# The step size's two halves: one read of PSUM each, and the absolute value made from the copy ahead of the exponent

## The chip, the core and the metric

The kernel runs on one core of one Trainium2 chip. The metric is the device time of one execution, in microseconds (us). Five engines work side by side, each through its own list of instructions in order: TensorE (PE in the profile; its weight loads are PEld), VectorE (DVE), ScalarE (ACT), GpSimd (POOL) and SyncE (SP), which issues most of the transfers. They wait for each other through semaphores.

## The reference

Input `x` is 32 sequences of 256 tokens with 128 channels. Each token goes through a mixture-of-experts layer, a selective-scan layer and the same mixture-of-experts layer again:

```
x = x + 0.5 * ffn(layernorm(x))
x = x + mamba(layernorm(x))
x = x + 0.5 * ffn(layernorm(x))

# in mamba
delta = softplus(x_conv @ W_dt + b_dt)            # 256 inner channels: the step size
dA    = exp(delta * A)                            # 16 states
h     = dA * h + (delta * x_conv) * B             # over the 256 tokens, one after the other
y     = sum over states of h * C, + D_skip * x_conv
```

`ffn` has 8 experts with hidden width 176, of which each token uses the best two, and a shared expert of width 352. The 256 inner channels of mamba lie on 128 partitions in two halves. softplus is computed as max(v, 0) + ln(1 + exp(-|v|)).

## The kernel before, in words

Two sequences (512 tokens) make a group, and there are 16 groups. The function `body(k, odd)` of every engine is one step of a software pipeline; k runs from -2 to 17. In step k group k is scanned; group k+1 goes through normalisation, projections, convolution and step size (the steps that `lead` lets in); group k+2 enters with its first ffn; and group k-1 leaves the scan and starts on its second. A step has 32 slots. The table `PLAN` says which named step stands in which slot, and every engine walks through the same table and takes its own part of each named step, so the table and the order of the `if`s within `body` are the order of each engine's list. In slot 2s VectorE scans state s of the 16 (L924, `hist`), from the decays that ScalarE made (L686, four instructions for two states) and from an input term that VectorE multiplied in PSUM (L876, `ps_db`) out of a row that TensorE spread there (L1058). GpSimd multiplies each `hist` by the row C (L623, `prod`), and one transfer per two states adds `prod` to `yacc` (L640). Between these stand 28 units of the two ffn passes: TensorE L1076 (`ps_h1a`, `ps_h1b` in turn), ScalarE's Silu L706, TensorE L1098 (`ps_h2`), VectorE's product L904 with a row of expert weights (`wrow`) that SyncE loads (L418), GpSimd's product L555, TensorE's down projection L1090. TensorE's matmul L1076 of a unit waits until the Silu two units earlier is done, since it writes the same bank. The second pass's last unit ends in VectorE's L911 (named step `addy1`, slot 21), which adds `ps_y` to `xres`; SyncE then stores the finished group (L384), waits until the store has landed, loads a new group (L376), and goes on with the expert rows.

A group's small products share one PSUM bank, `ps_m`. TensorE may write it only after the engine that last took it has counted up `misc_taken` (`claim`). Among these are `dt0` (slot 17) and `dt1` (slot 18), the two halves of the step size (L1141). ScalarE takes each half from the bank twice, and the second read gives the bank free:

```
774  nc.scalar.activation(dtmp[:, half, :], ps_m[:], ACT.Abs,
775                       bias=b_dt_c[:, half:half + 1]).then_inc(softplus_chain, 1)
776  nc.scalar.activation(dpre[:, half, :], ps_m[:], ACT.Identity,
777                       bias=b_dt_c[:, half:half + 1]).then_inc(misc_taken, 1)
```

In slot 20, behind the decays of states 12 and 13, comes `sp_exp`, which needs the same table of functions as the decays:

```
794  act.wait_ge(softplus_chain, (HALVES + 1) * (k + 2) - 1)
795  nc.scalar.activation(dtmp[:], dtmp[:], ACT.Exp, scale=-1.0).then_inc(softplus_chain, 1)
```

`sp_ln` (slot 22, L780) takes the logarithm, and VectorE joins `dpre` and `dtmp` to `delta` in slot 26 (L965). The units of the first ffn pass stand in slots 18 to 31, one in each, from position 0; position 3 is in slot 21 (`ps_h1b`), position 5 in slot 23 (`ps_h1b`). Slot 23 also holds the transposition of the normalised tokens for the second pass (`xT1`: TensorE L1037, ScalarE's copy L711), and slot 24 the routing product (`logits1`, TensorE L1110), which VectorE copies in slot 25 (L944) before it ranks the experts. In the first steps (k below 2) another table, `START_PLAN`, is used.

Of the kernel before, what the change touches and what calls it, by code (L numbers as in the profile page):

```python
# [17 lines left out]
def macaron_kernel(nc, x, W_in, b_in, conv_w, conv_b, W_xp, b_xp, W_dt, b_dt, A_log, D_skip, W_out, b_out,  # L18
# [6 lines left out]
    E, _, H = W1.shape  # L25
# [19 lines left out]
    NW = 4  # L45
# [31 lines left out]
    MISC_ENTRY = ["xT0", "logits0", "wT0"]  # L77
    MISC_LEAD = ["xT2", "in0", "in1", "in2", "in3", "dt0", "dt1", "xproj", "cT", "bT"]
    MISC_TAIL = ["outproj", "xT1", "logits1", "wT1"]
# [13 lines left out]
    def start(k):  # L93
        return isinstance(k, int) and k < FULL

    def plan(k):
        return START_PLAN if start(k) else PLAN

    def sp_plan(k):
        return START_SP if start(k) else SP_PLAN  # L100

    SETUP_MADE, SETUP_TAPS, SETUP_EDGE = 16, 24, 28

    def first(k):
        return isinstance(k, int) and k == -2

    def enters(k):
        return not isinstance(k, int) or 0 <= k + 2 < G

    def lead(k):  # L110
        return not isinstance(k, int) or 0 <= k + 1 < G

    def scans(k):
        return not isinstance(k, int) or 0 <= k < G

    def tail(k):
        return not isinstance(k, int) or 0 <= k - 1 < G

    def last(k):
        return not isinstance(k, int) or 0 <= k - 2 < G  # L120

    def misc_list(k):
        names = (enters(k) * MISC_ENTRY) + (lead(k) * MISC_LEAD) + (tail(k) * MISC_TAIL)
        return [n for s in range(SLOTS) for n in plan(k).get(s, []) if n in names]

    def before(k, names_of):

        if isinstance(k, int):
            return sum(len(names_of(i)) for i in range(-2, k))
        return sum(len(names_of(i)) for i in range(-2, FULL)) + (k - FULL) * len(names_of(FULL))  # L130

    def turn(k, name):

        return before(k, misc_list) + misc_list(k).index(name) + 1

    def turn_last(k, name):

        after = misc_list(k - 1 if isinstance(k, int) else FULL - 1)
        return before(k, misc_list) - (len(after) - 1 - after.index(name))

    def ffn_no(k, f):

        if isinstance(k, int) and k < FULL:
            return k + 2
        if isinstance(k, int) and k >= G - 2:
            return k + G - 2
        return 2 * k + 1 - f

    def route_no(k, step):

        if isinstance(k, int) and k < 1:
            return k + 2
        if isinstance(k, int) and k >= G - 2:
            return k + G - 1
        return 2 * k + (2 if step.endswith("1") else 1)

    def fcount(k, f, per, n):

        return ffn_no(k, f) * per + n

    def f_parity(k, f):
        return ffn_no(k, f) % 2 if isinstance(k, int) else 1 - f

    def w_turn(k, odd, f, e):

        if isinstance(k, int):
            n = ECHUNK * ffn_no(k, f) + e
            return n % NW, 2 * 16 * (n // NW + 1)
        n = ECHUNK * (2 * odd + 1 - f) + e
        return n % NW, 2 * 16 * (2 * ECHUNK // NW) * (k - odd) + 2 * 16 * (n // NW + 1) + (  # L170
            2 * 16 * (2 * ECHUNK % NW) // NW) * (k - odd)

    def unit(k, odd, slot, lag):

        back = slot < lag
        of, parity = (k - 1, 1 - odd) if back else (k, odd)
        units = START_UNIT if start(of) else UNIT
        if slot - lag + back * SLOTS not in units:
            return None
        f, pos = units[slot - lag + back * SLOTS]  # L180
        return (of, parity, f, pos) if (last(of) if f else enters(of)) else None

    def home(engine, group):

        return group % XS if isinstance(group, int) else engine.snap(group % XS)

    def iterations(engine, body):

        for k in range(-2, G + 2):
            body(k, k % 2)  # L190

    ctx = ExitStack()
    with ctx:
# [176 lines left out]
        def _(sp):  # L370
            def row_of(g):

                return g * NSEQ if isinstance(g, int) else sp.snap(g * NSEQ)
# [5 lines left out]
            def store(g, slot, first, k):  # L379

                sp.wait_ge(y_taken, ffn_no(k, 1) + 1)

                sp.wait_ge(x_loaded, 16 * min(g + XS, G) if isinstance(k, int) else 16 * (g + XS))
                sp.dma_start(out[bass.ds(first, NSEQ)].rearrange("b (t p) c -> p (b t) c", p=P),  # L384
                             xres[:, slot, :, :]).then_inc(x_stored, 16)
                sp.wait_ge(x_stored, 16 * (g + 1))

            def rows_c(g, par, p):
# [4 lines left out]
                if p > 1 or not isinstance(g, int) or g > 0:  # L393
                    sp.wait_ge(prod_done, NS * g + 2 * p - 2)
# [10 lines left out]
            def rows_w(k, odd, f, e, route=None):  # L405

                place, value = w_turn(k, odd, f, e)
                n = fcount(k, f, NCHUNK, e if e >= NW else e - (NCHUNK - ECHUNK))
                if not isinstance(n, int) or n > 0:
                    sp.wait_ge(h2_taken, n)  # L410
# [10 lines left out]
            def body(k, odd):  # L421
                for slot in range(SLOTS):
                    for step in sp_plan(k).get(slot, []):
                        if step[0] == "c" and scans(k):
                            rows_c(k, odd, int(step[1:]))
                        elif step == "next_c0" and lead(k):
                            rows_c(k + 1, 1 - odd, 0)
                        elif step == "store_w0" and enters(k) or step == "store_w1" and tail(k):
                            store_w(k, int(step[7]))
                        elif step[:3] == "w0:" and enters(k):  # L430
                            rows_w(k, odd, 0, int(step[3:]), route_no(k, "wT0"))
                        elif step[:3] == "w1:" and int(step[3:]) < NW and tail(k):
                            rows_w(k + 1, 1 - odd, 1, int(step[3:]), route_no(k, "wT1"))
                        elif step[:3] == "w1:" and int(step[3:]) >= NW and last(k):
                            rows_w(k, odd, 1, int(step[3:]))
                        elif step == "keep_x1n" and scans(k):
                            sp.wait_ge(norm_ready[2], k + 1)
                            if tail(k):
                                sp.wait_ge(mamba_added, k)
                            sp.dma_start(rtok[:], x1n[odd][:]).then_inc(x1n_ready, 16)  # L440
                        elif step == "store_x" and last(k):
                            at, stored, loaded = home(sp, k - 2), row_of(k - 2), row_of(k - 2 + XS)
                            store(k - 2, at, stored, k)
                            if not isinstance(k, int) or k - 2 + XS < G:
                                load(k - 2 + XS, at, loaded)
# [25 lines left out]
            iterations(sp, body)  # L471
# [3 lines left out]
        def _(pool):  # L475
# [39 lines left out]
            def norms_list(k):  # L515
# [681 lines left out]
```

## Time and profile before

| | us |
|---|---|
| median of 3 runs | 1838.47 |
| lowest, highest | 1837.09, 1841.13 |
| the profiled execution's own time | 1839.04 |
| its span in the trace | 1837.3 |
| TensorE busy | 1658.7 |
| VectorE busy | 1478.3 |
| GpSimd busy | 1445.7 |
| ScalarE busy | 1266.2 |

The granted clock of TensorE was 0.959 of full speed on average over the span. A timeline row has the start in us from the beginning of the span, the duration, the engine, the line of the kernel, what is written and read (partitions x elements), how many instructions were merged into the row, and in brackets the idle time of that engine before it and who ended it. A releaser is inferred from semaphore events.

### The profile page before, as it was taken

To read this page: it belongs to the slowest core of one execution; us is meant where nothing else is said; L and a number is where in the kernel's file an instruction comes from. 1 tells how busy PE (TensorE), PEld (TensorE's weight loads), DVE (VectorE), ACT (ScalarE), POOL (GpSimd) and SP (SyncE) were. 2 spreads that over 40 slices of the span, in tenths; PEclk is the share of its full clock that TensorE was granted. 3 is DMA by queue.
4 is the path that set the end of the run, shared out by engine and by line. 5 is a ranking of instruction groups with operands and counts; after the bars stand their busy time and mean duration, and the time that the engine had idled before them with its cause. 6 is when DMAs were issued, how large, how long until landed. Compare 5 with 4: busy or idle time off the path is not lost.

```text
span 1837.3 us, 24041 instructions
## 1 busy us (share of the span) xinstructions
PE 1658.7 (90%) x7378; PEld 1001.5 (55%) x7378; DVE 1478.3 (80%) x2241; ACT 1266.2 (69%) x2030; POOL 1445.7 (79%) x1366
## 2 busy tenths in 40 slices
PE   5898788999999999999999999999999999958488
PEld 3454445556555555656555555656555555534255
DVE  1438889989798988989798988989898998989732
ACT  2367678787877778776867777786877777665422
POOL 3336869888898988888888888888898888887753
PEclk9998889999999999999999999999999999969599
DMA  6026768687776868686777867777677868767642
GB/s 158 24 87 141 180 150 193 160 205 173 185 184 162 207 156 201 158 194 170 178 184 170 201 158 189 181 187 184 168 190 172 196 156 192 184 152 186 143 104 69
DMA packets 121287, 304.54 MB, mean 166 GB/s; under 512 B 19299, under 2 KB 40518, under 8 KB 106822
## 3 DMA queue, kind: packets, MB, share of 16 engines
q0 software_dynamic: 18432, 125.84, 34.4%
q1 hardware_dynamic: 98406, 174.46, 33.3%
q10 hardware_dynamic: 4320, 2.71, 0.5%
q8 instruction: 58, 0.95, 0.2%
q14 instruction: 71, 0.58, 0.1%
HBM read 167.67 MB, written 5.24 MB: 94 GB/s over the span
## 4 chain that ended last, share of the span: by engine, by line
POOL 43%; DMA 23%; issue 14%; PE 9%; DVE 7%; ACT 1%; SPq 1%; POOLq 0%; ACTq 0%; DVEq 0%
DMA yacc<-prod 19%; POOL prod L623 18%; POOL gated L555 14%; DVE hist L924 4%; DMA crow<-c_rows 3%; POOL yacc L619 2%; PE ps_y L1090 2%; DVE ps_db L876 2%; POOL yacc L640 1%; PE ps_h1a L1076 1%; SPq L418 1%; PE ps_h2a L1098 1%; PE ps_h1b L1076 1%; PE ps_h2b L1098 1%; POOL xres L610 1%
## 5 line engine op out<-in xcount | busy, mean ns | idle before, releaser
L623 POOL TENSOR_TENSOR prod<-hist,crow 128x1024 f32<-128x1024 f32 x224 | 556.5, 2484 | 204.7 <-DVE hist L924 171.0
L1090 PEld LDWEIGHTS ps_y<-down_w,gated 128*128 128x128 f32 (+1 forms) x3584 | 474.0, 196 | 276.4 <-issue 160.1
L924 DVE TENSOR_TENSOR_SCAN hist<-decay,ps_db 128x1024 f32<-128x1024 f32 x256 | 583.3, 2278 | 2.8
L555 POOL TENSOR_TENSOR gated<-gated,silu 128x512 f32<-128x512 f32 x352 | 493.3, 1450 | 74.4 <-DVE gated L904 71.4
L1090 PE MATMUL ps_y<-down_w,gated 128*128 128x128 f32 (+1 forms) x3584 | 491.8, 282 | 58.0 <-POOL gated L555 56.3
L876 DVE TENSOR_TENSOR ps_db<-du,ps_db 128x1024 f32<-128x1024 f32 x256 | 313.2, 1224 | 114.2 <-PE ps_db L1058 112.1
L686 ACT ACTIVATE decay<-delta,a_neg 128x510 f32<-128x510 f32 x512 | 326.8, 709 | 3.7 <-DVE delta L965 2.2
L706 ACT ACTIVATE silu<-ps_h1a 128x512 f32<-128x512 f32 (+1 forms) x224 | 132.9, 593 | 194.8 <-PE ps_h1a L1076 194.6
L1076 PE MATMUL ps_h1b<-xnT,up_w 128*128 128x512 f32 x448 | 236.7, 610 | 3.6 <-ACT silu L706 3.1
L1098 PE MATMUL ps_h2a<-xnT,up_w 128*128 128x512 f32 (+1 forms) x448 | 236.1, 609 | 1.9 <-DVE gated L904 1.9
L1076 PE MATMUL ps_h1a<-xnT,up_w 128*128 128x512 f32 (+1 forms) x448 | 236.4, 609 | 0.0
L1098 PE MATMUL ps_h2b<-xnT,up_w 128*128 128x512 f32 x448 | 232.0, 600 | 1.4 <-DVE gated L904 1.4
L904 DVE TENSOR_TENSOR gated<-ps_h2b,wrow 128x512 f32<-128x512 f32 x192 | 130.7, 681 | 60.3 <-PE ps_h2b L1098 40.2
L706 ACT ACTIVATE silu<-ps_h1b 128x512 f32<-128x512 f32 x224 | 133.0, 594 | 63.6 <-PE ps_h1b L1076 52.1
L686 ACT ACT_TABLE_LOAD x124 | 159.1, 1283 | 2.2
L904 DVE TENSOR_TENSOR gated<-ps_h2a,wrow 128x512 f32<-128x512 f32 x160 | 107.9, 674 | 46.3 <-PE ps_h2a L1098 36.2
L706 ACT ACT_TABLE_LOAD x111 | 142.4, 1283 | 2.0
L1058 PE MATMUL ps_db<-bT,sel_b 96*128 96x512 bf16 x256 | 102.2, 399 | 41.5 <-DVE hist L924 41.4
L1047 PE MATMUL ps_m<-xnT,w_conv 128*128 128x512 f32 (+3 forms) x256 | 118.2, 596 | 0.0
L1076 PEld LDWEIGHTS ps_h1a<-xnT,up_w 128*128 128x128 f32 (+1 forms) x448 | 85.0, 192 | 56.6 <-issue 47.0
L1076 PEld LDWEIGHTS ps_h1b<-xnT,up_w 128*128 128x128 f32 x448 | 79.1, 194 | 64.0 <-issue 37.5
L640 POOL DMA_DIRECT2D yacc<-prod x112 | 101.6, 908 | 1.6 <-issue 1.3
(136 smaller groups left out, 1937.5 us busy)
## 6 DMA issues: line engine op xcount, KB each, us to landing
yacc<-prod POOLq DMA_DIRECT2D x112, 1024.0 KB, 10.0
crow<-c_rows SPq DMA_DIRECT2D x128, 512.0 KB, 5.0
wrow<-w_rows SPq DMA_DIRECT2D x320, 128.0 KB, 6.3
wrow<-w_rows SPq DMA_DIRECT2D x64, 224.0 KB, 7.0
wrow<-w_rows SPq DMA_DIRECT2D x64, 192.0 KB, 6.4
wrow<-w_rows SPq DMA_DIRECT2D x64, 160.0 KB, 2.9
yacc<-yacc POOLq DMA_DIRECT2D x16, 512.0 KB, 7.8
wrow<-w_rows SPq DMA_DIRECT2D x64, 96.0 KB, 2.9
```

The costliest lines, as they stand in the source:

```text
L555: nc.gpsimd.tensor_tensor(gated[:, pos % NGATE, :], gated[:, pos % NGATE, :], silu[:, (pos + NCHUNK * f_parity(of, f)) % NSILU, :], ALU.mu ...
L623: nc.gpsimd.tensor_tensor(prod[:, (pair - 1 + odd) % 2, s % 2, :, :], hist[:, s % 2, :, :], c_all, ALU.mult).then_inc(prod_done, 1)
L640: pool.dma_start(yacc[odd][:], prod[:, (pair - 1 + odd) % 2, :, :, :], accum_op=ALU.add).then_inc(acc_done, 16)
L686: ins = nc.scalar.activation(decay[:, s % NA, half, :, 1:LEN], d[:, :, 1:LEN], ACT.Exp, scale=a_neg[:, half, s:s + 1])
L706: nc.scalar.activation(silu[0:r, (pos + NCHUNK * f_parity(k, f)) % NSILU, :], ps_h1[pos % 2][0:r, :], ACT.Silu).then_inc(silu_done, 1)
L876: nc.vector.tensor_tensor(ps_db[:].rearrange("p (h t) -> p h t", h=HALVES), du[par][:], ps_db[:, TG:2 * TG].unsqueeze(1).to_broadcast([P, ...
L904: nc.vector.tensor_tensor(gated[0:r, pos % NGATE, :], ps_h2[pos % 2][0:r, :], factor, ALU.mult).then_inc(h2_taken, 1)
L924: nc.vector.tensor_tensor_scan(hist[:, s % 2, :, :].rearrange("p h t -> p (h t)"), decay[:, s % NA, :, :, :].rearrange("p h b t -> p (h b ...
L1047: nc.tensor.matmul(acc[:, :, late:LEN], w_conv[:, tap, half * P:(half + 1) * P], now[:, :, 0:LEN - late], start=(tap == PAD), stop=False)
L1076: nc.tensor.matmul(ps_h1[pos % 2][0:r, :], up_w[:, 0, j * P:j * P + r], xnT[f][:], start=True, stop=True).then_inc(h1_full, 1)
L1090: ins = nc.tensor.matmul(ps_y[:, t * C:(t + 1) * C], gated[0:rd, posd % NGATE, t * P:(t + 1) * P], down_w[0:rd, jd, :], start=(posd == 0 a ...
L1098: nc.tensor.matmul(ps_h2[pos % 2][0:r, :], up_w[:, 1, j * P:j * P + r], xnT[f][:], start=True, stop=True).then_inc(h2_full, 1)
```

## The change

Each half of the step size is read from `ps_m` once, by the copy with the bias (`dpre`), which gives the bank free. The absolute value is made from `dpre` in SBUF for both halves in one instruction, in `sp_exp`, directly ahead of the exponent, and the exponent waits for it.

```
-                            nc.scalar.activation(dtmp[:, half, :], ps_m[:], ACT.Abs,
-                                                 bias=b_dt_c[:, half:half + 1]).then_inc(softplus_chain, 1)
                             nc.scalar.activation(dpre[:, half, :], ps_m[:], ACT.Identity,
                                                  bias=b_dt_c[:, half:half + 1]).then_inc(misc_taken, 1)
-                        elif step == "sp_ln" and lead(k):
-                            act.wait_ge(softplus_chain, (HALVES + 1) * (k + 2))
+                        elif step == "sp_ln":
+                            act.wait_ge(softplus_chain, 2 * (it + 2))
                             nc.scalar.activation(dtmp[:], dtmp[:], ACT.Ln, bias=1.0).then_inc(logterm_ready, 1)
...
-                    if "sp_exp" in plan(k).get(slot, []) and lead(k):
-
-                        act.wait_ge(softplus_chain, (HALVES + 1) * (k + 2) - 1)
-                        nc.scalar.activation(dtmp[:], dtmp[:], ACT.Exp, scale=-1.0).then_inc(softplus_chain, 1)
+                    for step, it in steps(k, slot):
+                        if step == "sp_exp":
+
+                            act.wait_ge(misc_taken, turn(it, "dt1"))
+                            nc.scalar.activation(dtmp[:], dpre[:], ACT.Abs).then_inc(softplus_chain, 1)
+                            act.wait_ge(softplus_chain, 2 * (it + 2) - 1)
+                            nc.scalar.activation(dtmp[:], dtmp[:], ACT.Exp, scale=-1.0).then_inc(softplus_chain, 1)
```

The rest of the diff rewrites how the tables are read: the counts that semaphores are compared with come from one list of all named steps in place of formulas, and branches for a register-held k are gone. The lists of TensorE, VectorE, GpSimd and SyncE are the same before and after, instruction by instruction and wait by wait, but for the line numbers. On ScalarE one wait is added beside those at the step size: the last `bounce` copy (`wT1` of the last step) also waits for `c_stored`.

ScalarE's list in slots 17 to 20 of a full step, before. L774 is the absolute value, L776 the copy, L795 the exponent; behind it come a table load and the Silu of position 3:

```order
L706 ACT_TABLE_LOAD
L706 ACTIVATE silu<-ps_h1b 128x512
L774 ACTIVATE dtmp<-ps_m,b_dt_c 128x512
L776 ACTIVATE dpre<-ps_m,b_dt_c 128x512
L706 ACTIVATE silu<-ps_h1a 128x512
L774 ACTIVATE dtmp<-ps_m,b_dt_c 128x512
L776 ACTIVATE dpre<-ps_m,b_dt_c 128x512
L706 ACTIVATE silu<-ps_h1b 128x512
L706 ACTIVATE silu<-ps_h1a 96x512
L686 ACT_TABLE_LOAD
L686 ACTIVATE decay<-delta,a_neg 128x2x255 x4
L795 ACTIVATE dtmp<-dtmp 128x1024
```

The same place in the changed kernel:

```order
L709 ACT_TABLE_LOAD
L709 ACTIVATE silu<-ps_h1b 128x512
L776 ACTIVATE dpre<-ps_m,b_dt_c 128x512
L709 ACTIVATE silu<-ps_h1a 128x512
L776 ACTIVATE dpre<-ps_m,b_dt_c 128x512
L709 ACTIVATE silu<-ps_h1b 128x512
L709 ACTIVATE silu<-ps_h1a 96x512
L692 ACT_TABLE_LOAD
L692 ACTIVATE decay<-delta,a_neg 128x2x255 x4
L796 ACTIVATE dtmp<-dpre 128x1024
L798 ACTIVATE dtmp<-dtmp 128x1024
```

Two instructions of 512 elements are gone ahead of the two copies, and one of 1024 elements (L796) stands between the decays and the exponent (L798). The number of table loads is the same over the whole list.

## Rows read from the trace of the kernel before

**Rows 1.** The page, part 1 (busy time) and part 4 (chain that ended last)
```profile
...
PE 1658.7 (90%) x7378; PEld 1001.5 (55%) x7378; DVE 1478.3 (80%) x2241; ACT 1266.2 (69%) x2030; POOL 1445.7 (79%) x1366
...
POOL 43%; DMA 23%; issue 14%; PE 9%; DVE 7%; ACT 1%; SPq 1%; POOLq 0%; ACTq 0%; DVEq 0%
...
```

**Rows 2.** Groups by line and shape, ScalarE: busy us, mean ns of one, idle before
```profile
...
L774 ACT ACTIVATE dtmp<-ps_m,b_dt_c 128x512 f32<-128x512 f32 x32 | 21.9, 684 | 26.9 <-PE ps_m L1141 26.9
...
L795 ACT ACTIVATE dtmp<-dtmp 128x1024 f32<-128x1024 f32 x16 | 16.7, 1042 | 0.0
...
```

**Rows 3.** Waits of the whole run: waiter, released by, total us, times, longest us
```profile
...
DVE gated L904 <- DMA wrow<-w_rows: 30.1, 19, 5.5
...
PE ps_m L1141 <- ACT dpre L776: 14.6, 14, 2.2
...
```

**Rows 4.** Timeline 989 to 1028 us, ScalarE: start, duration (us), instruction, [idle before <-releaser]
```profile
...
996.02 0.68 ACT L774 ACTIVATE dtmp<-ps_m,b_dt_c 128x512 f32<-128x512 f32 x1
996.59 0.69 ACT L776 ACTIVATE dpre<-ps_m,b_dt_c 128x512 f32<-128x512 f32 x1
...
1003.11 0.59 ACT L706 ACTIVATE silu<-ps_h1a 96x512 f32<-96x512 f32 x1 [1.94 <-PE ps_h1a L1076]
...
1005.01 2.55 ACT L686 ACTIVATE decay<-delta,a_neg 128x510 f32<-128x510 f32 x4
1007.47 1.04 ACT L795 ACTIVATE dtmp<-dtmp 128x1024 f32<-128x1024 f32 x1
1008.53 1.28 ACT L706 ACT_TABLE_LOAD   x1
1009.83 0.60 ACT L706 ACTIVATE silu<-ps_h1b 128x512 f32<-128x512 f32 x1
...
1016.61 0.59 ACT L711 ACTIVATE xnT<-ps_m 128x512 f32<-128x512 f32 x1
...
```

**Rows 5.** Timeline of the same stretch, TensorE's matmuls
```profile
...
997.43 1.96 PE L1141 MATMUL ps_m<-xconv,w_dt 128*128 128x512 f32 x4 [1.02 <-ACT dpre L776]
...
1010.99 1.02 PE L1076 MATMUL ps_h1b<-xnT,up_w 128*128 128x512 f32 x2
...
1014.04 0.38 PE L1058 MATMUL ps_db<-bT,sel_b 96*128 96x512 bf16 x1
...
1017.26 1.06 PE L1110 MATMUL ps_m<-wg,xnT 128*128 128x8 f32 x8 [0.22 <-ACT xnT L711]
...
1020.86 0.38 PE L1058 MATMUL ps_db<-bT,sel_b 96*128 96x512 bf16 x1
...
```

**Rows 6.** Timeline of the same stretch, VectorE
```profile
...
1007.50 0.69 DVE L911 SCALAR_TENSOR_TENSOR xres<-ps_y,xres 128x512 f32<-128x512 f32 x1 [0.66 <-PE ps_y L1090]
...
1014.46 1.23 DVE L876 TENSOR_TENSOR ps_db<-du,ps_db 128x1024 f32<-128x1024 f32 x1 [0.95 <-PE ps_db L1058]
...
1018.97 0.18 DVE L944 TENSOR_SCALAR logit<-ps_m 128x32 f32<-128x32 f32 x1
...
1022.05 1.22 DVE L876 TENSOR_TENSOR ps_db<-du,ps_db 128x1024 f32<-128x1024 f32 x1
...
1023.79 2.27 DVE L924 TENSOR_TENSOR_SCAN hist<-decay,ps_db 128x1024 f32<-128x1024 f32 x1
...
```

**Rows 7.** Timeline of the same stretch, GpSimd
```profile
...
1026.14 3.25 POOL L623 TENSOR_TENSOR prod<-hist,crow 128x1024 f32<-128x1024 f32 x1 [1.63 <-DMA yacc<-prod]
```

**Rows 8.** Timeline 895 to 925 us, VectorE and SyncE's queue, one step earlier
```profile
...
919.93 0.69 DVE L904 TENSOR_TENSOR gated<-ps_h2b,wrow 128x512 f32<-128x512 f32 x1 [2.59 <-DMA wrow<-w_rows]
...
902.16 0.41 SPq L384 DMA_DIRECT2D out<-xres  x1
908.76 0.39 SPq L376 DMA_DIRECT2D xres<-L_attn_x  x1
909.20 1.43 SPq L418 DMA_DIRECT2D wrow<-w_rows  x2
...
```

**Rows 9.** Timeline 495 to 505 us, VectorE, four steps before that
```profile
...
501.15 0.69 DVE L904 TENSOR_TENSOR gated<-ps_h2b,wrow 128x512 f32<-128x512 f32 x1 [1.33 <-DMA wrow<-w_rows]
...
```

More of the change, by code:

```diff
@@ L91, in macaron_kernel @@
     }
[L93 to L100, printed above, removed]
     SETUP_MADE, SETUP_TAPS, SETUP_EDGE = 16, 24, 28
-    def first(k):
-        return isinstance(k, int) and k == -2
+    PLANS = {k: START_PLAN for k in range(-2, FULL)}
+    UNITS = {k: START_UNIT for k in range(-2, FULL)}
+    SP_PLANS = {k: START_SP for k in range(-2, FULL)}
     def enters(k):
-        return not isinstance(k, int) or 0 <= k + 2 < G
+        return 0 <= k + 2 < G
@@ L126, in before @@
[L126 to L147, printed above, removed]
@@ L173, in unit @@
[L173 to L187, printed above, removed]
+        return 0 <= k - 2 < G
@@ new lines, in macaron_kernel, with at, steps, sp_steps @@
+    THERE = {name: role for role, names in ROLES for name in names}
+    def at(entry, k):
+        name, _, shift = entry.partition("@")
+        return name, k + int(shift or 0)
+    def steps(k, slot):
+        of = [at(entry, k) for entry in PLANS.get(k, PLAN).get(slot, [])]
+        return [(name, it) for name, it in of if THERE[name](it)]
+    def sp_steps(k, slot):
+        there = {"c": scans, "next_c0": lead, "store_w0": enters, "store_w1": tail, "w0": enters, "w1": last,
+                 "w1_first": tail, "keep_x1n": scans, "store_x": last}
+        of = [at(entry, k) for entry in SP_PLANS.get(k, SP_PLAN).get(slot, [])]
+        def kind(name):
+            if name[0] == "c":
+                return "c"
+            if name[:3] == "w1:" and int(name[3:]) < NW:
+                return "w1_first"
+            return name.partition(":")[0]
+        return [(name, it) for name, it in of if there[kind(name)](it)]
@@ new lines, in macaron_kernel @@
+    ALL = [(name, it) for k in range(-2, G + 2) for slot in range(SLOTS) for name, it in steps(k, slot)]
+    MISC = {step: n + 1 for n, step in enumerate(s for s in ALL if s[0] in MISC_NAMES)}
+    ROUTES = [(it, name[4]) for name, it in ALL if name in ("tilt0", "tilt1")]
+    STAT_STEPS = [s for s in ALL if s[0] in ("stats0", "stats1", "stats2", "stats3")]
+    BOUNCED = [s for s in ALL if s[0] in ("wT0", "wT1", "cT")]
+    UNIT_AT = {}
+    for k in range(-2, G + 2):
+        for slot, (f, pos, *shift) in UNITS.get(k, UNIT).items():
+            it = k + sum(shift)
+            if (last(it) if f else enters(it)):
+                UNIT_AT[(k + 2) * SLOTS + slot] = (it, f, pos)
@@ L422, in body @@
                 for slot in range(SLOTS):
[L423 to L445, printed above, removed]
@@ L707, in body @@
+                        nc.scalar.activation(silu[0:r, (pos + NCHUNK * f_parity(of, f)) % NSILU, :],
                                              ps_h1[pos % 2][0:r, :], ACT.Silu).then_inc(silu_done, 1)
-                    for step in plan(k).get(slot, []):
-                        if step == "xT0" and enters(k) or step == "xT1" and tail(k) or step == "xT2" and lead(k):
-                            take(k, step)
+                    for step, it in steps(k, slot):
+                        nxt, entering, ahead, behind = 1 - it % 2, home(it + 2), home(it + 1), home(it - 1)
+                        if step == "xT0" or step == "xT1" or step == "xT2":
+                            take(it, step)
@@ L1166, in body @@
                             ins.then_inc(misc_full, 1)
-                    if slot == SETUP_EDGE and first(k):
+                    if slot == SETUP_EDGE and k == -2:
                         make_edge()
```

452 lines of the change are left out of this document (234 added, 218 removed).

## The prediction

> **What bounds the kernel now.** I read the page first. No engine fills the span: TensorE is busy for 90% of it, VectorE 80%, GpSimd 79%, ScalarE 69% [rows 1]. In the chain that ended last GpSimd and transfers hold most, ScalarE 1% [rows 1]. That reads as if an edit on ScalarE could do nothing. But the chain leaves out who waits for a copy out of the shared bank, so I read the waits next: TensorE stood still 14 times, 14.6 us in all, until ScalarE's `dpre` (L776) gave `ps_m` free, so it could write the second half of the step size [rows 3]. Last I read one full step instruction by instruction (989 to 1028 us) on each engine [rows 4 to 7]. The steps are near copies of each other, so what holds there holds in most.
>
> In this step ScalarE starts the absolute value of the first half at 996.02, its copy at 996.59, and the copy ends at 997.28 [rows 4]. TensorE starts the second half at 997.43 after 1.02 us idle, 0.15 behind the copy [rows 5]. From there TensorE has no gap up to 1017.26. VectorE waits for it: 0.66 us for the last down projection ahead of L911, 0.95 for the row of state 12 [rows 6]. From 1014.46 VectorE is busy without a gap to the scan of state 13, which ends at 1026.06, and GpSimd has idled 1.63 us until that state's product [rows 6, 7]. The profile names a transfer as its releaser, but the product starts 0.08 behind the scan, and by the code waits for the scan alone. So in this stretch the step is paced by copy, then TensorE, then VectorE, then GpSimd.
>
> **What the change takes away.** Per step two absolute values of 0.684 us [rows 2]. Each takes 0.57 of ScalarE's time, from one start to the next [rows 4]. For TensorE only the first counts: `dpre` of the first half ends 0.57 earlier, and the wait of 1.02 falls to 0.45 [rows 5]. It isn't used up, so the whole 0.57 reaches TensorE. In front of the second half ScalarE waits for TensorE anyway, so its absolute value hides under ScalarE's next wait, 1.94 us for position 2 [rows 4]; costed at nothing, and without that idle time it would be worth another 0.57.
>
> TensorE and all that waits for it (L911, the rows of states 10 and 11) now come 0.57 earlier. This lasts up to position 5, at 1010.99.
>
> **What it adds.** One absolute value of 1024 elements from SBUF. The trace of before has none; the nearest row is the exponent, of the same shape, both sides in SBUF, 1.042 us [rows 2]. Bounds: 0.68, one old instruction, as if twice the elements cost nothing more, and 2 x 0.684 = 1.37, the two old ones end to end. I take 1.04. The exponent must wait for its result. A handover from an ACTIVATE to a following one isn't in the trace either. Lower bound 0.02, the gap between the exponent's end (1008.51) and the table load behind it (1008.53) [rows 4]; upper bound 0.15, from the end of `dpre` to the matmul on another engine [rows 4, 5]. I take 0.07, near the 0.08 from the scan to GpSimd's product [rows 6, 7]. So everything on ScalarE behind the exponent comes 1.04 + 0.07 = 1.11 later, counted from the Silu of position 2, and that Silu comes 0.57 earlier, since it waits for TensorE.
>
> Here a page speaks against the change. The Trainium skill, "ScalarE: Activation LUTs", section What ACT_TABLE_LOAD costs, gives some 1.38 us of drain beside a table load. If a result that the next ACTIVATE needs cost such a drain, the handover would be 1.38 and not 0.07. The trace has 0.02 us before the load and 0.02 behind it, so it doesn't bear it out; what it would make of the time is a rival below. The sum doesn't use it.
>
> **Where the two meet.** The Silu of position 3 (1009.83 to 1010.43) releases TensorE's position 5, at 1010.99 [rows 4, 5]. That Silu's end moves by 1.11 - 0.57 = +0.54, to 1010.97. With the same 0.15 the matmul can start at 1011.12. TensorE, there 0.57 earlier at 1010.42, now stands still for 0.70. So the gain is given back within one step: position 5 starts 0.13 later than before, and so does the row of state 12 (1014.04), which VectorE waits for, and so the scan of state 13 and GpSimd. The next place is the copy L711 at 1016.61, for which TensorE already waits 0.22 [rows 4, 5]: it moves by 0.54, and so do L1110 (end 1018.32, now 1018.86) and the row of state 13 (end 1021.24, now 1021.78). VectorE asks for them at 1018.97 and 1022.05 [rows 6], so they are still hidden, by 0.11 and 0.27, and VectorE itself comes 0.13 later. If that cover went, ranking the experts would be late next.
>
> So a plain step costs **+0.13 us**. There are seven.
>
> **Steps with a late row of weights.** In five of the twelve full steps in the middle, VectorE waits at position 7, right ahead of the scan of state 13, for a row of expert weights: from 1.33 to 2.59 us [rows 8, 9], part of the 30.1 us of such waits in the run [rows 3]. There TensorE's 0.13 is covered. The row is late because SyncE issues it behind a store: the store goes out at 902.16, right behind L911; its landing releases the load at 908.76; the row goes out at 909.20 and lands at about 919.9 [rows 8]. L911 waits for TensorE [rows 6] at a point where TensorE is 0.57 earlier. So store, load and row come 0.57 earlier, if the transfers take as long as before: **-0.57 us** in each of five steps.
>
> **Sum.** 7 x 0.13 - 5 x 0.57 = 0.91 - 2.85 = -1.9. At both ends of the run two more steps have the wait of L1141 without this pattern: the 14.6 us less the twelve times 1.02 leave 2.4 us for both [rows 3, 5]. I take half of 0.57 for each, -0.6. In all -2.5. The profiled execution took 1839.04, so 1836.5; it lies 0.6 above the median of the three runs, so against that I forecast **1836.0 us**, -0.13%. What a measurement of this kernel can tell from no change is about 0.2%, 3.7 us.
>
> **Rivals.**
> (a) The gain in transfers is larger. A shift of 0.57 between the stores and the large accumulations changes what they share the DMA engines with, and the late rows may come in time altogether. For it: seven steps have no such wait, with the same instructions, so little decides. Against: nothing says it goes one way. If three of five waits of some 2 us vanish: -6, and with the rest 1830.5 us. Faster.
> (b) The transfers go the other way, slower. The store goes out 0.57 earlier while the accumulation beside it doesn't move, so it may land no earlier, while the next accumulation (after state 11's product) is issued 0.57 earlier, ahead of the expert row. Place: position 7 in the plain steps. It decides from the point where the row lands behind the end of the state-13 input term; the smallest such wait seen is 1.33 [rows 9]. Four of seven plain steps: +5.3, and nothing gained in the five: 1838.5 + 0.9 + 5.3 = 1844.7.
> (c) The transfers don't move. Then only the plain steps count: 12 x 0.13 at most, +1.6, less the 0.6 at the ends: 1839.5. Same.
> (d) ScalarE must come to rest before an instruction that needs the last one's result, for as long as a table load lasts, 1.28 [rows 4]. Then the handover is 1.21 more than I take, position 5 starts 1.34 later, a plain step costs that, a late one nothing: seven make +9.4, with the ends 1847.3 us. Slower. The 0.02 us on either side of the table load speak against it. (In the Trainium skill, ScalarE: Activation LUTs, it would be the drain of 1.38.)
> (e) The change doesn't do what it says: the wait of L1141 doesn't shrink, since TensorE has something else to finish. But its gap there is 1.02 us, more than 0.57 [rows 5], so I give this almost nothing; position 5 would then start 1.11 - 0.41 = 0.70 later, seven times, 1843.4.
>
> **Chances.** Forecast 0.46, (a) 0.22, (b) 0.11, (c) 0.16, (d) 0.03, (e) 0.02. The forecast lies 1.2 us from the border of faster, and the runs shown differ by 4 us; a fifth of it, 0.09, goes over. So faster 0.31, with (a). Slower is (b), (d) and half of (e), 0.15. Within 0.2%: 0.54. The range runs from 1829.5, just past (a), to 1843, which takes in (c) and part of (b); the bounds of the two new costs move a plain step from -0.23 (0.68 and 0.02) to +0.54 (1.37 and 0.15), which is -2.5 to +2.9 us for seven, inside it.
>
> **What would show it.** L1141's wait near 0.45 in full steps, the sum of row 3 from 14.6 to about 8. An absolute value of 1.04 and the exponent 0.02 to 0.15 behind its end. A new wait of TensorE for the Silu L706 of about 0.7 at position 5. The store 0.57 earlier against the state-9 product, and late rows shorter by 0.57. ScalarE busy down by 32 x 0.684 - 16 x 1.042 = 5.2 us. I am wrong if the first two don't hold; if they hold and the time is still off by more than 4 us, the transfers' step failed.

## The result

| | before | changed |
|---|---|---|
| median of 19 runs each, us | 1838.75 (1836.42 to 1844.11) | 1844.98 (1840.60 to 1850.41) |
| ratio to before, with 95% interval | | 1.0031 (1.0020 to 1.0042) |
| span of the profiled execution compared here, us | 1837.3 | 1844.8 |
| granted clock, mean | 0.959 | 0.963 |

The change made the kernel slower by 0.31%. I had forecast 1836.0 and a range up to 1843.0: wrong in sign, and just outside the range. In the page of the changed kernel (below) TensorE, VectorE and GpSimd have as many instructions as before, and ScalarE has 16 fewer, 32 old ones less 16 new ones [rows 1]. So the rewritten tables brought no instruction in on these engines. A kernel before with the edit on ScalarE alone was not run.

The page of the changed kernel, busy time and the chain that ended last, against [rows 1]:

```profile
PE 1656.8 (90%) x7378; PEld 998.7 (54%) x7378; DVE 1475.8 (80%) x2241; ACT 1265.7 (69%) x2014; POOL 1444.4 (78%) x1366
...
POOL 44%; DMA 23%; issue 15%; PE 11%; DVE 3%; ACT 2%; SPq 1%; POOLq 0%; ACTq 0%; DVEq 0%
```

Nothing there says where 7.5 us went. The groups of ScalarE, with columns as in [rows 2], and then the waits, with columns as in [rows 3], do better:

```profile
L776 ACT ACTIVATE dpre<-ps_m,b_dt_c 128x512 f32<-128x512 f32 x32 | 21.9, 684 | 28.1 <-PE ps_m L1136 28.1
...
L798 ACT ACTIVATE dtmp<-dtmp 128x1024 f32<-128x1024 f32 x16 | 16.9, 1057 | 0.5
L796 ACT ACTIVATE dtmp<-dpre 128x1024 f32<-128x1024 f32 x16 | 16.7, 1041 | 0.0
```

```profile
DVE gated L898 <- DMA wrow<-w_rows: 26.3, 15, 5.5
...
PE ps_m L1105 <- ACT xnT L715: 11.3, 18, 0.7
...
PE ps_h1b L1070 <- ACT silu L709: 9.3, 26, 1.5
...
PE ps_m L1136 <- ACT dpre L776: 6.7, 13, 1.6
```

The wait for `dpre` fell from 14.6 to 6.7 us, and a wait for the Silu came in. One of these lines misleads: VectorE's waits for rows of weights fell from 30.1 to 26.3 us over the run. What counts is where they stand. Read step by step, the waits at position 7, ahead of the scan of state 13, are five in before (1.33 to 2.59 us, 9.2 us in sum) and eleven of twelve now (0.59 to 2.79, 16.5 in sum). The waits for rows at the next position shrank, but they cost little: steps of before with 0.3 to 1.8 us of such a wait are as long (103.1 to 103.3 us) as the steps of experiment 1, which have none (103.27).

The profiled spans differ by 7.5 us. The twelve full steps hold 4.3 of it (1244.2 us before, 1248.4 now, from exponent to exponent), the start 2.6, the end 0.6. The 4.3 come, to within 0.1, out of two terms: 7.3 us more at position 7, less twelve times 0.24, since the step without a late row got shorter (experiments 1 and 2). I don't put the start's 2.6 down to the change: over the thirteen profiles of this study it varies by ten (the exponent of the first full step starts between 376.6 and 386.5 us).

**The mechanism in one step.** First a full step of before with its row in time: SyncE's queue (store, load, expert row), GpSimd's accumulations of states 8 and 9 and of 10 and 11, and VectorE at position 7 (start, duration, instruction).

```profile
1216.43 0.41 SPq L384 DMA_DIRECT2D out<-xres  x1
1222.80 0.39 SPq L376 DMA_DIRECT2D xres<-L_attn_x  x1
1223.24 0.96 SPq L418 DMA_DIRECT2D wrow<-w_rows  x2
...
1211.02 0.90 POOL L640 DMA_DIRECT2D yacc<-prod  x1
...
1223.45 0.93 POOL L640 DMA_DIRECT2D yacc<-prod  x1
...
1231.40 0.68 DVE L904 TENSOR_TENSOR gated<-ps_h2b,wrow 128x512 f32<-128x512 f32 x1
```

The same step of the changed kernel:

```profile
1218.42 0.41 SPq L394 DMA_DIRECT2D out<-xres  x1
1225.19 0.39 SPq L386 DMA_DIRECT2D xres<-L_attn_x  x1
1225.63 0.96 SPq L428 DMA_DIRECT2D wrow<-w_rows  x2
...
1213.56 0.89 POOL L646 DMA_DIRECT2D yacc<-prod  x1
...
1225.44 0.93 POOL L646 DMA_DIRECT2D yacc<-prod  x1
...
1236.59 0.69 DVE L898 TENSOR_TENSOR gated<-ps_h2b,wrow 128x512 f32<-128x512 f32 x1 [2.79 <-DMA wrow<-w_rows]
```

Count from the first accumulation. The store goes out 5.41 us behind it before and 4.86 now: 0.55 earlier, as forecast. But its landing, which releases the load, comes 11.78 behind it before and 11.63 now; over the twelve steps it lies between 11.5 and 12.7 in both kernels, 11.96 in the mean before and 11.98 now. The second accumulation, behind state 11's product, does move: 12.43 before, 11.88 now. So in before the row goes out 0.21 us ahead of a transfer of 1 MB, and now 0.19 behind it, and VectorE waits 2.79 us.

The row goes out in two pieces of 128 KB, mostly 0.54 us apart, and VectorE needs both. The trace of the changed kernel, for the two pieces of this step alone:

```profile
DMA to landing us min/median/max: 2.7/6.5/10.3
```

The first piece takes 2.7 us and the second 10.3, to 1236.47, which is 0.12 ahead of VectorE's start. In the step of before the second piece landed at 1230.98, in time.

### The profile page after: what moved, and what is told of

It reads as the page before. It is cut to its first block, busy times and chain, and to the rows that moved or that the text cites. A ratio compares the mean times of both kernels' runs of the same rounds, so it can differ in the third digit from the quotient of the medians.

```text
span 1844.8 us, 24025 instructions
## 1 busy us (share of the span) xinstructions
PE 1656.8 (90%) x7378; PEld 998.7 (54%) x7378; DVE 1475.8 (80%) x2241; ACT 1265.7 (69%) x2014; POOL 1444.4 (78%) x1366
## 4 chain that ended last, share of the span: by engine, by line
POOL 44%; DMA 23%; issue 15%; PE 11%; DVE 3%; ACT 2%; SPq 1%; POOLq 0%; ACTq 0%; DVEq 0%
DMA yacc<-prod 21%; POOL prod L629 17%; POOL gated L560 14%; POOL yacc L625 3%; PE ps_y L1084 3%; DVE hist L918 1%; POOL yacc L646 1%; PE ps_h1a L1070 1%; PE ps_h2b L1092 1%; PE ps_h1b L1070 1%; PE ps_h2a L1092 1%; DMA crow<-c_rows 1%; POOL xres L616 1%; POOL prob L583 1%; DVE ps_db L873 1%
```

## Experiments

Ratios are against runs of the kernel before on the same chip, with 95% intervals. "Late" counts full steps, of twelve, with a wait of VectorE at position 7 (in four of them the profile names TensorE, but in these too the last piece of the row lands 0.13 us or less ahead of VectorE's start). Such counts come from the one profiled execution of each kernel, the ratios from all.

**1 and 2. The row freed from the store.** SyncE's wait for the store's landing, and the load behind it, move behind the row of the following chunk, in before (`b_split`) and in the changed kernel (`a_split`).

```
-        ... 22: ["store_x"], 23: ["w0:4", "c7"], 24: ["w0:5"], ...
+        ... 22: ["store_x"], 23: ["w0:4", "c7"], 24: ["w0:5", "load_x"], ...
-                sp.wait_ge(x_stored, 16 * (g + 1))
+                        elif step == "load_x":
+                            sp.wait_ge(x_stored, 16 * (it - 1))
```

> The kernel before, with one thing changed on SyncE: the store of the finished group is no longer followed at once by the wait for its landing and the load of a new group. Both stand behind the expert rows of chunks 4 and 5, two slots later. Theory T (the expert row of chunk 4 lands late whenever SyncE issues it behind GpSimd's accumulation of states 10 and 11, and that wait of VectorE ahead of the scan of state 13 is what the change makes more frequent): the row goes out ahead of that accumulation in every step, the waits of VectorE for it (five steps, 1.3 to 2.6 us) vanish, and with them 9.8 us, the sum by which the product at position 7 starts later there than the 15.72 behind the exponent of the plain steps: 1838.8 - 9.8 = 1829. Rival R (the change is slower because the new absolute value makes ScalarE late for TensorE, and transfers have nothing to do with it): nothing on ScalarE or TensorE changes, so 1838.8, give or take 2.

> The changed kernel with the same edit on SyncE (the wait for the store's landing and the load of a new group stand behind the expert rows of chunks 4 and 5). T: the late rows, ten steps of twelve after the change, are gone, and what is left is the prediction's own sum for plain steps, about +0.1 per step: 1829 + 12 x 0.11 = 1830.5, within 3 us of the kernel before with the same edit. R: still 6 us slower than that one, about 1845 if the edit does nothing.

Measured: `b_split` 0.9946 (0.9931 to 0.9962), 1830.8 us; `a_split` 0.9929 (0.9911 to 0.9946), 1825.6 us. No late row at position 7 in either. SyncE's queue and GpSimd in `a_split`, where the row goes out 4.8 us ahead of the accumulation:

```profile
1201.46 0.41 SPq L394 DMA_DIRECT2D out<-xres  x1
1203.66 1.85 SPq L427 DMA_DIRECT2D wrow<-w_rows  x2
...
1208.47 0.94 POOL L648 DMA_DIRECT2D yacc<-prod  x1
```

With the rows in time a full step is 103.27 us in `b_split` and 103.02 in `a_split`. So here the change is worth -0.24 us a step, and the late rows are what turned it into a loss. A store that holds up a row behind it costs the kernel before 0.5%, the changed one 1.0%.

**3. The row made late in the kernel before** (`b_late`): the expert row is issued behind the row of C.

```
-        ... 23: ["w0:4", "c7"], 24: ["w0:5"], ...
+        ... 23: ["c7"], 24: ["w0:4", "w0:5"], ...
```

> The kernel before, with the expert row of chunk 4 issued behind the next pair of C rows (which waits for the product of state 11) instead of ahead of it, so that it always goes out at or behind the accumulation of states 10 and 11. Nothing on ScalarE changes. T: the seven full steps without a late row get one, 1.3 to 2.8 us each, about 2.0 in the mean, +14, and the five others stay: 1853, at least 1846. R: nothing happens to ScalarE, so 1838.8, give or take 2.

Measured: 1.0158 (1.0139 to 1.0176), 1868.7 us. The row is behind the accumulation in all twelve steps, and late in all twelve, by 2.3 to 4.3 us. The direction is theory T's, the size more than its 1853: the waits at position 7 sum to 37.3 us, where I had priced them from the 1.3 to 2.6 us of before. The edit does one thing more than it was meant to: the row of C, 512 KB, now goes out ahead of the expert row on SyncE's queue. How much of the 2.3 to 4.3 us that adds wasn't tested.

**4. The absolute value per half, right behind each copy** (`a_half`). The bank comes free as early as in the changed kernel; the exponent waits for less.

```
+                            act.wait_ge(misc_taken, turn(it, step))
+                            nc.scalar.activation(dtmp[:, half, :], dpre[:, half, :], ACT.Abs).then_inc(softplus_chain, 1)
...
-                            act.wait_ge(misc_taken, turn(it, "dt1"))
-                            nc.scalar.activation(dtmp[:], dpre[:], ACT.Abs).then_inc(softplus_chain, 1)
-                            act.wait_ge(softplus_chain, 2 * (it + 2) - 1)
+                            act.wait_ge(softplus_chain, 3 * (it + 2) - 1)
                             nc.scalar.activation(dtmp[:], dtmp[:], ACT.Exp, scale=-1.0).then_inc(softplus_chain, 1)
```

> The changed kernel with the absolute value made for each half by itself, from the copy in SBUF, right behind that copy (a wait of ScalarE for its own copy is added). So the bank is given free as early as in the changed kernel, but the exponent has nothing new ahead of it, as in the kernel before. T: position 5 of TensorE follows 0.57 earlier than before, but the accumulation of states 10 and 11 is early too and the store's landing isn't, so the expert row stays late in about ten steps, and that wait sets the scan of state 13: 1844, between 1841 and 1846. R: ScalarE is no longer late, so faster than before by up to 12 x 0.57 = 6.8: 1832.

Measured: 1.0044 (1.0027 to 1.0062), 1848.0 us, 2 above theory T's upper bound, with eleven late rows. ScalarE's late exponent is not what costs the time, since without it nothing is won. TensorE's early start is enough.

**5 and 6. The accumulation held back, nothing else.** One (`a_hold`) or three (`a_hold3`) small additions on GpSimd ahead of the accumulation of states 10 and 11 in the changed kernel. They add work and put nothing back of the old order on ScalarE. The edit of `a_hold3`:

```
+                if pair == 5 and k >= FULL:
+                    for r in range(3):
+                        if k > FULL or r > 0:
+                            pool.wait_ge(held, 3 * (k - FULL) + r)
+                        nc.gpsimd.tensor_tensor(holder[:], alpha_b[:], beta_b[:], ALU.add).then_inc(held, 1)
                 ticket((PAIRS + 1) * k + pair - 1)
                 pool.dma_start(yacc[odd][:], prod[:, (pair - 1 + odd) % 2, :, :, :], accum_op=ALU.add
```

> The changed kernel with one small addition of 128 x 64 elements on GpSimd right ahead of the accumulation of states 10 and 11, in every full step, so that this accumulation is issued about as late as before the change, and nothing else is put back. Theory T (the accumulation, issued 0.6 to 1.1 us earlier against the exponent, goes ahead of the expert row that waits for the load): in most steps the row is issued ahead of the accumulation again, position-7 waits of VectorE over 1.3 us fall from ten to about five, time 1838.5 us (1836 to 1842). Rival R (it is ScalarE's later exponent, or the earlier store, that costs the time, not this order): the late rows stay, 1845 us or, with the added 0.45 us on GpSimd, up to 1850.

> The changed kernel with three small additions instead of one on GpSimd ahead of the accumulation of states 10 and 11: each moved it by 0.42 us in the run with one, so it goes out at about 7.95 us behind the exponent's start, where the kernel before had 7.77 and the changed kernel 6.69; the expert row goes out at 6.4 to 8.2. Nothing of ScalarE's order is put back. Theory T (a row issued behind the accumulation is always late, one issued ahead of it seldom): at most two or three steps have the row behind, three to five late rows of the twelve full steps, and with the faster plain step of 103.0 us 1834 to 1839 us. Rival R (the exponent's or the store's place makes the rows late): nine or more late rows, 1844 us or above.

Measured: `a_hold` 1.0008 (0.9990 to 1.0025), 1844.1 us with nine late rows. I had expected 1838.5 and five: by its time and its count this run is nearer to rival R. The addition (128x128 elements, not the 128x64 that I had written down) had moved the accumulation by 0.42 us only, and in seven steps the row was still behind. That is why `a_hold3` was run: 0.9962 (0.9948 to 0.9977), 1832.8 us, a little below theory T's 1834 to 1839, with three late rows (1.25, 0.89 and 0.09 us). GpSimd and SyncE in `a_hold3`:

```profile
1215.58 1.52 POOL L651 TENSOR_TENSOR holder<-alpha_b,beta_b 128x128 f32<-128x128 f32 x3
...
1217.19 0.93 POOL L653 DMA_DIRECT2D yacc<-prod  x1
...
1215.54 0.39 SPq L388 DMA_DIRECT2D xres<-L_attn_x  x1
1215.98 0.96 SPq L430 DMA_DIRECT2D wrow<-w_rows  x2
```

Here 1.5 us more work per step on an engine that is busy for 80% of the span makes the kernel 0.7% faster than the changed one. GpSimd's idle time ahead of the product of state 13 takes the work up: 0.48 us of it is left in this step. And it isn't the row's own time that counts: counted from the exponent, seven rows of the changed kernel went out at +6.8 to +7.4 and all were late, nine of `a_hold3` at +6.6 to +7.4 and none was. The accumulation stood at +6.7 or +6.8 in the one and at +8.2 in the other. That is the plainest proof that its place against the row decides.

**7. Both lateness terms at once** (`a_both`): the old absolute value out of the bank comes back as an extra read ahead of each copy, and the new one stays.

```
+                            nc.scalar.activation(dtmp[:, half, :], ps_m[:], ACT.Abs,
+                                                 bias=b_dt_c[:, half:half + 1]).then_inc(extra_read, 1)
                             nc.scalar.activation(dpre[:, half, :], ps_m[:], ACT.Identity,
```

> The changed kernel with the old absolute value out of the bank put back as an extra read ahead of each half's copy, so that the bank comes free as late as before, while the exponent still waits for the new absolute value of both halves. Nothing is left out. Theory T (the rows are late because what TensorE's earlier start moves, the accumulations, comes earlier, while the exponent comes later): TensorE waits 1.0 us for dpre again, position 5 starts 1.1 us - 0.41 = 0.7 us later than before the change, but the accumulation stands against the store's landing as before, so about five late rows: between 1838.8 + 12 x 0.7 = 1847 if nothing hides it and 1843 if the state-12 product leaves half of it hidden. Rival R (ScalarE's later exponent alone makes the rows late): ten late rows and the 0.7 us on top, 1851 us or more.

Measured: 1.0016 (0.9998 to 1.0034), 1844.7 us, five late rows, and TensorE's wait for `dpre` back at 14.7 us. A step without a late row is 103.6 to 103.7 us. Here TensorE is late and ScalarE too, and by these runs it is no slower than the changed kernel.

The kernels without the split, in one table. "Gap" is the time between the issues of the two accumulations (median of twelve); "behind" counts the steps in which the row's first piece goes out after the second accumulation.

| kernel | gap, us | row behind | late | waits at position 7, us | ratio |
|---|---|---|---|---|---|
| `a_half` | 11.84 | 10 | 11 | 18.0 | 1.0044 |
| changed | 11.86 | 11 | 11 | 16.5 | 1.0031 |
| `a_hold` | 12.27 | 7 | 9 | 14.0 | 1.0008 |
| `a_both` | 12.43 | 3 | 5 | 5.4 | 1.0016 |
| before | 12.44 | 4 | 5 | 9.2 | 1 |
| `a_hold3` | 13.34 | 0 | 3 | 2.2 | 0.9962 |

With `b_late` (12 behind, 12 late) the row went out behind the accumulation in 47 steps and was late in all 47; it went out ahead in 37 and was late in 9. The second piece tells more. Where it was issued 0.5 to 2.2 us behind the accumulation, the row was late in 52 steps of 52; where it was issued earlier than that, in 4 of 32. In [rows 8], one of the five late steps of before, the first piece goes out 0.09 us ahead of the accumulation, but SyncE takes 1.43 us for the two in place of 0.96, so the second stands 0.93 behind, and the wait is the 2.59 us. The late second pieces landed 0.3 us ahead to 2.3 us behind the accumulation's own landing, but for three of `a_hold3`; those in time landed 2.3 us or more ahead of it.

The landing of the store stayed between 11.3 and 12.8 us behind the first accumulation in all seven kernels, with means of 11.9 to 12.0, whether the store went out 5.4 us behind it or 4.8. No run moved that accumulation by itself, so what holds the landing there isn't shown.

**8 to 11. What sets a step whose rows come in time.** Experiments 1 and 2 left a question: I had forecast +0.13 us for such a step, and it was -0.24. In the trace VectorE's comparison `hot` for the experts, only 128x64, takes 1.80 us in before and 1.12 in the changed kernel, and both times it ends 0.08 to 0.09 us behind GpSimd's product of state 12. Before, then changed:

```profile
1227.91 2.35 POOL L623 TENSOR_TENSOR prod<-hist,crow 128x1024 f32<-128x1024 f32 x1
...
1228.55 1.80 DVE L959 TENSOR_TENSOR hot<-lanes,topi 128x64 f32<-128x64 f32 x1
```

```profile
1229.90 2.36 POOL L629 TENSOR_TENSOR prod<-hist,crow 128x1024 f32<-128x1024 f32 x1
...
1231.22 1.12 DVE L954 TENSOR_TENSOR hot<-lanes,topi 128x64 f32<-128x64 f32 x1
```

To test it, GpSimd's join of slot 24 is put behind that product, so the product runs 1.2 us earlier (0.5 in the changed kernel, where it then starts right behind the scan of state 12): in `b_split` (`b_split_pf`), in `a_split` (`a_split_pf`), and in `a_half` with the split (`a_half_split_pf`; `a_half_split` is the same without this edit).

```
+                    joins = u is not None and ORDER[u[2]] < ECHUNK
+                    behind_product = slot == 24 and k >= FULL and k < G
+                    if joins and not behind_product:
+                        join(u)
...
                                 accumulate(k, odd, pair)
+                    if joins and behind_product:
+                        join(u)
```

> The kernel before with the load taken out of SyncE's way, and GpSimd's join of slot 24 put behind the state-12 product, which then comes some 1.2 us earlier. Theory T (VectorE's comparison for the experts, 128 x 64 with two inputs from SBUF, stands still while GpSimd's product runs, 1.79 us for what takes 1.12 when the product comes earlier): the comparison falls to 1.1 us or less and a full step of 103.2 us to about 102.5, time 1830.8 - 12 x 0.7 = 1822 us (1819 to 1826). Rival R (the length of the comparison has nothing to do with the product, or the scan of state 13 waits for something else): step 103.2 or, with the join late, more, 1830.8 us or above.

> The changed kernel with both edits: the load out of SyncE's way, and GpSimd's join of slot 24 behind the state-12 product. Theory T (product and comparison pull at each other): the product comes earlier by some 1.2 us as in the kernel before with both edits, whose full step is 102.5; but here position 5 and the row of state 12 are up to 0.67 us later against the store's accumulation, so the step is 102.4 to 102.8 and the time 1819 to 1823 us. Rival R (in the changed kernel the comparison is already at 1.12 us, so nothing is left to win): step 103.0, 1825.6 us.

> Absolute values made from the copies, one per half right behind each copy, and the load taken out of SyncE's way, so that no row is late. Theory T (with the rows in time the step goes by ScalarE, TensorE, VectorE, GpSimd): the exponent waits for one half less of the absolute value than in the changed kernel, a full step is between 102.4 and 103.0 us, time 1818 to 1825.6 us. Rival R (the end of the step is set by the state-12 product and the VectorE work around it, whatever ScalarE does): step 103.0, time 1825.6 +- 1.5 us.

> Both edits, with absolute values made from the copies, one per half, right behind each copy: the bank comes free as early as in the changed kernel and the exponent waits for one half only, already done. Theory T (both terms of the change are gone from the path and the comparison is not stretched): a full step of 102.2 to 102.5 us, below both the kernel before with these edits (102.5) and the changed one, time 1815 to 1819.7 us. Rival R (TensorE's 0.57 us at the bank's copy is given back at the next wait, whatever is done on ScalarE): step 102.5 to 102.7, 1819.7 to 1823 us.

Measured, with the length of a full step (mean of nine):

| | before, split | changed, split | per half, split |
|---|---|---|---|
| join as it was | 103.27 us, 0.9946 | 103.02, 0.9929 | 102.72, 0.9896 (0.9865 to 0.9928) |
| join behind product | 102.54, 0.9871 (0.9841 to 0.9901) | 103.04, 0.9937 (0.9921 to 0.9954) | 101.94, 0.9855 (0.9840 to 0.9870) |

The product and `hot` in `b_split_pf`:

```profile
1007.66 2.38 POOL L630 TENSOR_TENSOR prod<-hist,crow 128x1024 f32<-128x1024 f32 x1
...
1009.46 0.66 DVE L968 TENSOR_TENSOR hot<-lanes,topi 128x64 f32<-128x64 f32 x1
```

Again it ends 0.08 us behind the product, and the step is 0.73 shorter; theory T had 0.7. In the changed kernel the same edit gives nothing, as rival R said. But R's reason, that nothing is left to win at `hot`, isn't it: `hot` fell from 1.12 to 0.65 us there too, and position 7 still started 14.96 us behind the exponent, as in `a_split` and in `b_split_pf`. So from there on the step goes by the exponent. How late that is shows in the scan of state 15, counted from the second half of the step size. TensorE and VectorE in `b_split_pf` and then in `a_split_pf`:

```profile
986.54 1.96 PE L1150 MATMUL ps_m<-xconv,w_dt 128*128 128x512 f32 x4 [1.03 <-ACT dpre L785]
...
1024.73 2.27 DVE L933 TENSOR_TENSOR_SCAN hist<-decay,ps_db 128x1024 f32<-128x1024 f32 x1
```

```profile
986.40 1.95 PE L1145 MATMUL ps_m<-xconv,w_dt 128*128 128x512 f32 x4 [0.43 <-ACT dpre L785]
...
1025.67 2.27 DVE L927 TENSOR_TENSOR_SCAN hist<-decay,ps_db 128x1024 f32<-128x1024 f32 x1
```

38.19 us against 39.27: the exponent's lateness (1.07) arrives whole, the 0.6 won at the bank goes off, and 0.50 a step is left. So with nothing else in the way the change costs half a microsecond a step, and the absolute value per half wins 0.6. That `a_split_pf` is 0.66% above `b_split_pf` is more than the 0.3% that 12 times 0.50 make. The two were run on different chips, and the runs of `a_split_pf` lie between 1823 and 1832 us; I can't say where the rest is.

`a_half_split_pf`, at 1813.3 us, beats both kernels, by 1.45 and about 1.8%. Its step of 101.94 us and its time lie below what theory T had for it (102.2 and 1815 at the least).

## Why the prediction was wrong

**The failed step** is the one on the steps with a late row: "So store, load and row come 0.57 earlier, if the transfers take as long as before". The store came 0.55 earlier, and its landing did not. The term was -2.85 us; in its place the waits at position 7 grew by 7.3 us. I had written the condition down, and had priced the other case as rival (b) at a chance of 0.11. The profile of before held a warning. The row's margin over the accumulation was 0.09 to 0.76 us in eight steps and negative in four, and the accumulation was to come 0.57 earlier. Had I listed those twelve margins, I would have seen that everything hung on whether the landing follows the store. Before alone can't tell that, since its store stands 5.2 to 5.4 us behind the first accumulation in every step; the changed kernel can.

**Rival (b)** is what happened, in place (position 7 in steps that were plain) and in kind (a store that lands no earlier, an accumulation ahead of the row). Its price was four waits of 1.33 us, 5.3; it was six more waits and 7.3 us. Its time, 1844.7, is 0.3 from the median, and that is luck: it adds 0.9 for plain steps, which in fact gave back twelve times 0.24, and 2.6 us of the difference of the two profiles lies in the start, of which I can't say where it comes from.

**TensorE's wait** for `dpre` was to go from 1.02 to 0.45 us, and the sum from 14.6 to about 8: 0.42 to 0.46 in eleven full steps (0.24 in one, where before had 0.83), and 6.7. Right. The waits at the two ends fell by 0.43 and 0.57; whether the -0.6 that I took for them reached the time can't be told, as the start varies by more.

**The new absolute value** at 1.04 and a handover of 0.07: 1.04, and 0.03 from its end to the exponent. ScalarE in the changed kernel, against [rows 4]:

```profile
1217.67 1.04 ACT L796 ACTIVATE dtmp<-dpre 128x1024 f32<-128x1024 f32 x1
1218.74 1.06 ACT L798 ACTIVATE dtmp<-dtmp 128x1024 f32<-128x1024 f32 x1
1219.82 1.28 ACT L709 ACT_TABLE_LOAD   x1
1221.11 0.60 ACT L709 ACTIVATE silu<-ps_h1b 128x512 f32<-128x512 f32 x1
```

Right, and rival (d) is out: nothing drains in between. If a result that the next ACTIVATE needs cost the drain of 1.38 us that the Trainium skill, ScalarE: Activation LUTs, What ACT_TABLE_LOAD costs, gives beside a table load, the exponent would by estimate have started at about 1220.1.

**Position 5** was to start 0.13 later. TensorE, against [rows 5]:

```profile
1207.63 1.95 PE L1136 MATMUL ps_m<-xconv,w_dt 128*128 128x512 f32 x4 [0.46 <-ACT dpre L776]
...
1221.76 1.12 PE L1070 MATMUL ps_h1b<-xnT,up_w 128*128 128x512 f32 x2 [0.41 <-ACT silu L709]
...
1224.91 0.38 PE L1053 MATMUL ps_db<-bT,sel_b 96*128 96x512 bf16 x1
...
1228.54 1.06 PE L1105 MATMUL ps_m<-wg,xnT 128*128 128x8 f32 x8 [0.63 <-ACT xnT L715]
```

Counted from the second half of the step size, position 5 is at +13.56 before and at +14.13 now. Less the 0.57, that is 0.00. TensorE loses 0.57 there from start to start and not 0.70, mostly since the matmul starts 0.05 behind the Silu and not 0.15. The profile shows 0.41 of it as idle, because the matmul ahead (1220.33, 1.02 us) would have overlapped this one by 0.16. The row of state 12 is at +17.28 for +16.61, so 0.10 later, near the +0.13 that I had.

**The plain step**, though, was not +0.13 but -0.24. From this row to VectorE I had assumed that a delay passes on. It didn't: `hot` ended with GpSimd's product, whenever it started. The product comes with the early part of the step, 0.57 earlier, and so does the end of `hot`. Of the row of state 13 I had said that it is still hidden, by 0.27: it wasn't. VectorE now waits 0.23 us for it, and reaches that input term at +24.94 in place of +24.62 [rows 5, 6]: 0.32 later, less 0.57, is -0.25. That term was mis-sized by 0.37 us a step, 4.4 us in the run, in the change's favour. So the forecast missed by less than its failed step alone would make it. One of its bounds was off too: 0.68 and 0.02 make a plain step -0.28 and not -0.23, which leaves the range as it was.

**ScalarE's busy time** was to fall by 5.2 us; it fell by 0.5. I had multiplied by the duration, 0.684, where start to start is 0.57 and the rest overlaps the next instruction. 32 x 0.57 is 18.2, against 16.7 of the new one, which leaves 1.5; the last 1.0 I can't place. This changes no other term.

## What to carry to other kernels

Where a store or a load and a small row stand close to a large transfer from another queue, list for each step which is issued first and by how much, and go by the row's last piece. If margins are below what the change shifts, the change can reorder them, and here that outweighed the gain by which it was judged. A shift on a path with slack must also be followed to the transfers that hang on its engine. And take a wait for a landing out from in front of urgent transfers: here that was worth more (0.5 to 1.0%) than the whole edit on ScalarE.

## What the runs showed of the hardware that I had not expected

- Here the store's landing didn't follow its issue. With the store 4.6 to 5.4 us behind a 1 MB accumulation it landed 11.3 to 13.1 us behind that accumulation in all thirteen profiles. An issue 0.6 us earlier (`a_split` against `b_split`) moved the mean landing from 12.02 to 11.98.
- A row of 256 KB in two pieces, issued 0.1 to 1.4 us behind an accumulation from another queue, was late in 47 of 47 steps; issued ahead of it, in 9 of 37. With the second piece 0.5 to 2.2 us behind it was late in 52 of 52, otherwise in 4 of 32, and the late second pieces, but for three, landed 0.3 us ahead to 2.3 us behind the accumulation's own landing. How the engines share between the queues in those microseconds stays open.
- A VectorE instruction of 128x64 took 0.66, 1.12 or 1.80 us by when GpSimd's product started, and ended 0.08 behind it each time; in `a_hold3`, where it starts 0.15 ahead of the product, it takes 0.23 to 0.29. This agrees with the Trainium skill, SBUF — State Buffer, SBUF: two separate sides, by which a VectorE operation with two SBUF inputs and a GpSimd operation that reads SBUF exclude each other for a whole instruction.
